# Self product as a fifth seven-block relation, first products run between the norms, projection splits on GpSimd

## What is computed

```python
def layer0(h):
    h = h @ W + b; adj = symmetric 0/1 matrix of the edges + eye, rows divided by their sums
    cur, out = h, w[0] * h
    for i in range(3):
        cur = adj @ cur
        out = out + w[i + 1] * cur
    return relu(out)

def layer1(x):
    total = sum over r of (x[src] @ W_rel[r] + b_rel[r]) * (weight where edge_type == r)
    agg = segment_sum(total, dst) / max(deg, 1)
    h = x @ W_self + b_self + agg
    x1 = layer_norm(x + h) * g1 + be1
    return layer_norm(x1 + gelu(x1 @ W1 + b1) @ W2 + b2) * g2 + be2

x = x + layer0(relu(norm(x)))
x = x + layer1(relu(norm(x)))
x = x + layer2(relu(norm(x)))     # one graph convolution
x = x + layer3(relu(norm(x)))     # two mean-aggregating convolutions
```

## Time and profile before

| | us |
|---|---|
| median of three runs | 345.9 |
| the profiled execution's own time | 345.88 |
| its span in the trace | 343.6 |
| TensorE matmul busy | 336.5 (98%) |
| VectorE busy | 243.2 (71%) |
| GpSimd busy | 153.0 (45%) |
| ScalarE busy | 87.1 (25%) |

### The profile page before, as it was taken

The page is one execution under the profiler, slowest core; times in us unless marked ns, Lnnn a source line. Parts: engine busy times, 40 slices in busy tenths (PEclk is TensorE's granted clock), DMA queues, the critical chain, the costliest instruction groups (busy, mean ns, idle before and its releaser), DMA issues.

```text
span 343.6 us, 4413 instructions
## 1 busy us (share of the span) xinstructions
PE 336.5 (98%) x1624; PEld 239.5 (70%) x1625; DVE 243.2 (71%) x428; ACT 87.1 (25%) x187; POOL 153.0 (45%) x122
## 2 busy tenths in 40 slices
PE   7999999999999999999999999999999999999996
PEld 3459887785478888888888888844774544474455
DVE  5899999988596898691484598786676555443543
ACT  3565664333410000000001062223352331112110
POOL 6000000461379999999936220491115440772020
PEclk9999999999999999999999999999999999999999
DMA  7100002728800000062300089942000000000003
GB/s 240 66 1 2 5 2 85 284 57 216 279 0 2 0 1 0 2 245 65 59 0 2 0 283 190 139 141 73 1 2 0 1 0 0 2 0 0 2 0 124
DMA packets 18630, 22.07 MB, mean 64 GB/s; under 512 B 2032, under 2 KB 10992, under 8 KB 18608
## 3 DMA queue, kind: packets, MB, share of 16 engines
q1 hardware_dynamic: 17936, 20.72, 21.6%
q0 software_dynamic: 240, 0.79, 0.8%
q10 hardware_dynamic: 432, 0.26, 0.2%
HBM read 20.72 MB, written 1.05 MB: 63 GB/s over the span
## 4 chain that ended last, share of the span: by engine, by line
PE 88%; DVE 8%; ACT 1%; DMA 1%; issue 1%; ACTq 0%; DVEq 0%
PE bank L1887 14%; PE bank L1736 14%; PE bank L1679 14%; PE bank L1616 8%; PE bank L1776 7%; PE bank L1843 6%; PE bank L1927 4%; PE bank L603 4%; PE bank L576 4%; PE bank L1875 4%; PE bank L600 3%; PE bank L1603 2%; PE bank L592 2%; DMA bias<-in_edge_type 1%; DVE stats L1209 1%; DVE h L1241 1%
## 5 line engine op out<-in xcount | busy, mean ns | idle before, releaser
L1051 ACT ACTIVATE columns<-mean_var,eps 128x1 f32<-128x1 f32 x16 | 4.7, 292 | 109.4 <-DVE mean_var L1210 109.3
L1736 PE MATMUL bank<-slots,wall 128*128 128x256 f32 x128 | 30.2, 380 | 0.0
L603 PE MATMUL bank<-slots 128*128 128x112 bf16 x256 | 27.8, 228 | 0.0
L907 POOL TENSOR_TENSOR slots<-slots 128x512 f32<-128x512 f32 x1 | 1.3, 1293 | 58.7 <-DMA slots<-in_L_gnn_W_rel 58.7
L1736 PEld LDWEIGHTS bank<-slots,wall 128*128 128x128 f32 x128 | 24.2, 190 | 3.2
L600 PE MATMUL bank<-slots 128*128 128x140 bf16 x128 | 26.2, 242 | 0.0
L386 DVE TENSOR_TENSOR slots<-slots 128x1792 bf16<-128x1792 bf16 (+1 forms) x27 | 25.0, 979 | 0.0
L1679 PE MATMUL bank<-slots,h_t 128*128 128x256 f32 x104 | 24.5, 380 | 0.0
L603 PEld LDWEIGHTS bank<-slots 128*128 128x128 bf16 x256 | 22.5, 103 | 2.7
L1887 PE MATMUL bank<-wall,h_t 128*128 128x512 f32 x48 | 22.4, 596 | 0.4 <-ACT slots L1160 0.4
L1679 PEld LDWEIGHTS bank<-slots,h_t 128*128 128x128 f32 x104 | 19.7, 190 | 3.1 <-issue 0.5
(11 more groups left out here) (293 smaller groups left out, 799.6 us busy)
## 6 DMA issues: line engine op xcount, KB each, us to landing
slots<-in_L_gnn_W_rel SPq DMA_DIRECT2D x4, 1024.0 KB, 9.6
spare<-in_L_gnn_W_ffn SPq DMA_DIRECT2D x1, 2048.0 KB, 8.0
slots<-in_L_gnn_W_ffn SPq DMA_DIRECT2D x1, 2048.0 KB, 9.1
slots<-in_L_gnn_Wr SPq DMA_DIRECT2D x8, 256.0 KB, 9.1
x<-in_x SPq DMA_DIRECT2D x4, 256.0 KB, 5.7
bias<-in_L_gnn_W SPq DMA_DIRECT2D x2, 512.0 KB, 5.0
slots<-in_L_gnn_W_self SPq DMA_DIRECT2D x1, 1024.0 KB, 5.3
bias<-in_L_gnn_b_rel SPq DMA_DIRECT2D x4, 256.0 KB, 8.4
```

The lines of the kernel that those rows point to most:

```text
L603: ins = pe.matmul(place[:, :, 0:R, 0:WIDE].rearrange("p h r d -> p r h d"), low, wgt_hot[:, s, v, a, :, :, j], start=False, stop=False, sk ...
L1736: ins = pe.matmul(into, left[:, k, tile(p)], right[:, k, :], start=(n in (0, 2, 3, 5) and r == 0 and k == 0), stop=False, skip_group_check ...
```

## The change

- The self product becomes relation 0 of five (`RELS = R + 1`), made from seven block products like the others; its result goes to a new buffer `own_out`, which shares its memory with `cnt_r`. VectorE adds it to `h` at the end of the relations (four instructions, `own_added`), and ScalarE's copies into `cnt_r` wait for that. `bself` is added as a relation's bias, so GpSimd's four additions go, and so do the four `keep_self`.
- Of the first three relations (`AHEAD = 3`) P1 and P2, which need node tiles 0 and 1 only, run on TensorE between the transposes of tiles 1, 2 and 3; `first_half(q, m)` is P1 for one output tile. Each has a bank of its own (0, 1, 2), and they share banks 3, 6 and 7 for the rest. The rest has the order P5, P6, P7, P4, P3 for relation 0 and P6, P7, P5, P4, P3 for 1 and 2. VectorE takes P1 out with `keep_right(q)`: for 0 and 1 behind tile 2's norm, for 2 behind tile 3's.
- `split_projection` of tiles 1, 2 and 3 moves from VectorE to GpSimd (`proj_split`), ahead of `combine_rel(0)`; VectorE waits for all three ahead of the inverse row sums.
- `combine_rel(0)` is now that of `wself`, whose load is the first of the three, and writes to slot 0 instead of 7. `combine_rel(1)` to `(4)` follow behind the node sums in a new order with `add_weights` and `combine_messages`.
- In the third hop `(0, 3)` is done one place earlier; `add_hop(2, 3)` stands behind tile 0's scale and shift instead of ahead of it.
- The degree product moves from the end of pass `r == 1` to the end of pass `r == 3`.
- The rows of `bself` and `brel` are loaded ahead of the five other rows.

```diff
@@ hops and projection splits @@
-                split_projection(1)
...
+            pool.wait_ge(late_kept, LATE_COUNTS)
+            for m in range(1, NT):
+                pool.wait_ge(proj_out, m + 1)
+                pool.tensor_tensor(lo[0][:, m, :], h[:, m, :], hi[0][:, m, :].bitcast(F32), ALU.subtract).then_inc(proj_split, 1)
             combine_rel(0)
             finish_build()
-            pool.wait_ge(rows_loaded, 16 * 6)
-            for t in range(NT):
-                pool.wait_ge(t_ready, use_of(H_REL, t) + 1)
-                pool.tensor_tensor(h[:, t, :], h[:, t, :], bself, ALU.add).then_inc(self_biased, 1)
             pool.wait_ge(hop_ready, HOPS * NT)
-            pool.wait_ge(node_s_ready, 3)
+            pool.wait_ge(node_s_ready, SUMS)
...
-            for t in range(2):
-                symmetric(t)
-            for t in range(2, NT):
+            for t in range(NT):
                 symmetric(t)
-                split_projection(t)
+            dve.wait_ge(proj_split, NT - 1)
             dve.wait_ge(adj_ready, NT)
...
-                    order = [(0, 0), (0, 1), (0, 2), (1, 0), (1, 1), (0, 3), (1, 2), (1, 3)]
+                    order = [(0, 0), (0, 1), (0, 2), (1, 0), (0, 3), (1, 1), (1, 2), (1, 3)]
@@ norm behind the hops, VectorE @@
+            def keep_right(q):
+
+                dve.wait_ge(rel_rows_loaded, 16 * RELS)
+                dve.wait_ge(msg_ready, rel_made(q, P1))
+                dve.tensor_tensor(quarter(rel_out[q], 0, 1), rel_parts(q)[0], rel_sides(q)[1], ALU.add).then_inc(msg_out, 1)
...
                 moments(TO_REL, m, x[:, m, :])
+                scale_and_shift(TO_REL, m)
                 if m == 0:
                     add_hop(HOPS - 1, NT - 1)
-                scale_and_shift(TO_REL, m)
+                if m == 2:
+                    keep_right(0)
+                    keep_right(1)
+            keep_right(2)
@@ relations, TensorE @@
-            pe.wait_ge(wself_loaded, 16)
-            for m in range(NT):
-                transposed(H_REL, m)
-                pairs = rows_by(wself, m)
-                product(main[m][:], pairs[:KT - 1], stop=False)
-                if m + 1 < NT:
-                    fill_h(H_REL, m + 1, h_ready[TO_REL])
-                product(main[m][:], pairs[KT - 1:], start=False).then_inc(self_ready, 1)
...
+            pe.wait_ge(acc_ready, HOPS * NT + 1)
+            for q in range(2):
+                pe.wait_ge(wrel_loaded[q], 16)
+            transposed(H_REL, 0)
+            first_half(0, 0)
+            first_half(1, 0)
+            fill_h(H_REL, 1, h_ready[TO_REL])
+            pe.wait_ge(wrel_loaded[2], 16)
+            first_half(2, 0)
+            transposed(H_REL, 1)
+            first_half(0, 1)
+            first_half(1, 1)
+            fill_h(H_REL, 2, h_ready[TO_REL])
+            first_half(2, 1)
+            second(0)
+            second(1)
+            fill_h(H_REL, 3, h_ready[TO_REL])
+            second(2)
+            for q in range(RELS):
...
+                    elif n == P4:
+                        pe.wait_ge(msg_out, rel_step(q, 3))
+                        pe.wait_ge(rel_t_ready, 4 * q + 4)
+                        block_product(p74, a22, t4, False)
@@ aggregation @@
-                if r == 1:
+                if r == R - 1:
                     pe.wait_ge(wgt_add, NT * (R - 1) + 3)
@@ GpSimd, behind the node sums @@
+            combine_rel(1)
+            combine_rel(2)
             add_weights(1)
+            combine_rel(3)
...
-            combine_rel(2)
+            add_weights(2)
+            combine_rel(4)
             combine_messages(0)
-            add_weights(2)
-            combine_rel(3)
             combine_messages(1)
             add_weights(3)
             combine_messages(2)
+            combine_messages(3)
@@ the end of the relations, VectorE @@
+            for t in range(NT):
+                dve.tensor_tensor(h[:, t, :], h[:, t, :], own_out[:, t, :], ALU.add).then_inc(own_added, 1)
```

More of the change, by code:

```diff
@@ L59 @@
 GROUPS = 4
+RELS = R + 1
+AHEAD = 3
 ADDS = 8
@@ L98, in gnn_program @@
             cnt_b = between.enter_context(nc.sbuf_tensor("cnt_b", [P, NT, N], BF16))
+        with ExitStack() as between:
+            own_out = between.enter_context(nc.sbuf_tensor("own_out", [P, NT, D], F32))
         cnt_r = sb("cnt_r", [P, NT, N], F32R)
@@ L1665, in _ @@
                         hop(m, s)
-            pe.wait_ge(wself_loaded, 16)
-            for m in range(NT):
-                transposed(H_REL, m)
-                pairs = rows_by(wself, m)
-                product(main[m][:], pairs[:KT - 1], stop=False)
-                if m + 1 < NT:
-                    fill_h(H_REL, m + 1, h_ready[TO_REL])
-                product(main[m][:], pairs[KT - 1:], start=False).then_inc(self_ready, 1)
-            def block_product(bank, left, right, fresh):
-                for m in range(2):
-                    for k in range(2):
-                        ins = pe.matmul(bank[:, m * HALF:(m + 1) * HALF], left[:, k, tile(m)], right[:, k, :],
-                                        start=fresh and m == 0 and k == 0, stop=False, skip_group_check=True)
-                ins.then_inc(msg_ready, 1)
@@ L1683, in _, with half_product @@
             a11, a12, a21, a22 = (quarter(h_t, j, i) for i in range(2) for j in range(2))
             s1, s2, s4 = node_s
-            for r in range(R):
-                b11, b12, b21, b22 = (quarter(wrel[r], i, j) for i in range(2) for j in range(2))
-                t1, t2, t4 = rel_t[r]
-                before, now = STEPS * (r - 1), STEPS * r
-                if r == 2:
+            def half_product(bank, left, right, m, fresh):
+                for k in range(2):
+                    ins = pe.matmul(bank[:, m * HALF:(m + 1) * HALF], left[:, k, tile(m)], right[:, k, :],
+                                    start=fresh and m == 0 and k == 0, stop=False, skip_group_check=True)
+                return ins
@@ new lines, in block_product, with first_half, second @@
+            def block_product(bank, left, right, fresh):
+                half_product(bank, left, right, 0, fresh)
+                half_product(bank, left, right, 1, fresh).then_inc(msg_ready, 1)
+            def first_half(q, m):
+                ins = half_product(rel_bank[q][0], a11, quarter(rel_weight[q], 0, 0), m, True)
+                if m == 1:
+                    ins.then_inc(msg_ready, 1)
+            def second(q):
+                pe.wait_ge(msg_out, rel_step(q, 1))
+                block_product(rel_bank[q][0], a12, quarter(rel_weight[q], 1, 0), False)
```

225 lines of the change are left out of this document (119 added, 106 removed).

## The result

The changed kernel takes 352.35 us (median of 4 runs, 351.40 to 354.67) against 346.02 before (4 runs), a ratio of 1.0192 with a 95% interval of 1.0141 to 1.0244. Forecast were 348.3 us and a range of 346.6 to 350.2. The kernel is slower, as forecast, but by 6.3 us instead of 2.4.

The account below looks back on a forecast made before the run. TensorE was taken as the bound (98% busy), except VectorE ahead of hop 2. From 345.9: +2.7 (steps 1, 2), -0.65, -2.0, +2.4, +0.1 give 348.4; following the clock through gave 348.3, which was taken; range 346.6 to 350.2 us.

Parts of the forecast that it names:

- Step 1: Start of the hops: three splits moved to GpSimd let VectorE start `weigh_projection` at 61.77 instead of 62.02; 0.25 us gained.
- Step 2: Ahead of hop 2: GpSimd's `combine_rel(0)` runs beside `weigh_projection` and blocks three of VectorE's four weighings; 3.0 us lost.
- no blocking: Rival ahead of hop 2: weighings go ahead of GpSimd or end before the load lands; no loss, 345.3 us; chance 12%.
- a smaller block: Rival ahead of hop 2: load lands 0.5 later, only two weighings blocked; 347.3 us; counted inside the main case's 72%.
- Step 3: Behind hop 3: earlier pair (0, 3) and later `add_hop(2, 3)` bring the first transpose at 80.02, not 80.67; 0.65 us gained.
- Step 4: TensorE's work: sixteen matmuls of 512 columns go, twenty-eight of 256 come; 2.0 us gained.
- 5a to 5f: Waits added at tile 1, the `h_t` copy, tiles 2 and 3, P7 to P4 of relation 0, degree product; 2.4 us lost.
- Step 5f: Degree product: its readers stand right behind it, so it takes 1.54 us with the wait instead of 0.92; 0.62 lost.
- Work hidden: Added work claimed to have cover, such as four `own_added` additions in idle VectorE time; GpSimd's sums close, 0.1 us charged.
- GpSimd late: Rival at the degrees: GpSimd's last weight sum comes behind `combine_messages(3)` and TensorE waits; 350 to 351 us; chance 6%.
- the clock falls: Rival in the pause ahead of hop 2: TensorE's clock drops to 1.2 GHz, up to 3.7 us more, 350 to 352; 10%.
- main case: Whole kernel: two to three weighings blocked, waits 0.6 either way; 346.9 to 349.0 us; chance 72%.

## Why the prediction was right and wrong

- **Step 1, splits on GpSimd: right.** Three in 3.77 us, 1.26 each. The weighings start at 61.84 (61.77 forecast).
- **Step 2, three blocked weighings: right**, 2.91 us instead of 2.7 at source tile 3 of hop 2. The rivals *no blocking* and *a smaller block* are wrong: 3.08 us is three blocked. The rule of the Trainium skill that stood beside it (SBUF — State Buffer, "Who interferes with whom") holds for VectorE's queued, independent instructions too, at a price of 1.04 for each. That is less than the 1.29 of a GpSimd instruction alone. So by these times the lock is not for the whole of both.
- **Step 3: right.** The first transpose is 2.28 us later (82.95 against 80.67), that is 0.63 gained, with 0.65 forecast.
- **Step 4 and 5a to 5f: nearly right.** The transposes come 3.76, 3.18 and 4.97 us apart, as the forecast clock has them (3.76, 3.16, 4.91). P4 of relation 0 starts 0.94 late (0.92 forecast), 0.78 of it listed as a wait, and the degree product takes 1.45 (1.54). But to the start of `p = 1` the loss is 3.57 where 2.3 was forecast. Of the 1.2 missing 0.2 are step 2. The relations, from the first transpose on, are 1.2 longer than forecast: 0.1 are the transposes, 0.1 the slower product behind the wait in relation 0, 0.8 the wait in relation 2, and 0.2 I can't place. The first half of the aggregation, with the degree product, is 0.2 shorter than forecast. The wait in relation 2 has no term in step 5: the step looks at TensorE's order, and finds P5 as cover between P7 and P4, but not that VectorE has `sum_weights(0, 0)`, at 1.64 beside GpSimd's new `combine_rel(3)`, ahead of both steps. The run with the sum moved shows it.
- **Step 5f and "Work hidden": the step that failed.** 5f priced the moved degree product as a wait of TensorE, 0.62 (0.50 measured). It did not follow what stands behind the degrees on VectorE: the whole of `p = 0`'s steps, norms and out-degrees. The paragraph on hidden work asked of each added instruction whether it had cover, not of the moved wait who was queued behind it. It also followed GpSimd only to its last sum of the weights (173.28, with 0.8 to spare, so that the rival *GpSimd late* is wrong), and not to its next instructions, which VectorE then meets. The runs showed 2.58 us lost there, in `p = 1`, to which the sum gave nothing: in the trace (32.83 instead of 30.25 us), and in two runs that take it away in different ways. What the paragraph did name as hidden was hidden: the four `own_added` took 6.77 us without a wait behind them. Its sum for GpSimd is slightly off: 95.8 and 47 times 1.5 and 4 are 170.3, not 169.9, and so behind the 170.05 and not ahead of it. GpSimd's time from the first to the last of these sums came out as worked out, 74.35 us.
- **The rival "the clock falls": right, in a part of the executions.** It had 10% as a case of its own, with 350 to 352. The runs show it not as a case of its own but as a chance in each run, added to the main case; the sum gave it nothing. Of the changed kernel's nine runs five are below 1.0, and the profiled one is not, so that the sum of its trace ends 0.95 short of the median. The estimate of 8 to 16 pairs at 0.92 came from no row; the one profile with a fall has seven at 0.86, which cost 2.4 us at the first transpose instead of up to 3.7. The advice of the Trainium skill against long pauses that was quoted with it (TensorE: Matmul & The Clock Gate, "Why this matters for your kernels") is borne out by the runs with the pause filled: none of 10 is below 1.0. But the pause brings the fall only in a part of the executions: 2.85 us cost nothing in one profile and a fall in another.

The sum with the measured terms starts from the 2.3 us forecast for the start of `p = 1`. To it come 0.2 in step 2, 1.2 in the relations, 0.2 less in the first half of the aggregation, and 2.6 in `p = 1`. Behind that 0.15 less are lost (6.15 us late at 208.37, 6.0 at the end of the span), and around the span 0.5 less. That makes 5.5, as between the two profiled executions (5.52). The other 0.95, up to the median, are put down to the clock, by the steps between the runs and by the runs with the pause filled; the one run of 350.43 shows that it is not the only thing that varies.

## What to carry to other kernels

When a wait is moved to a later place, list everything queued behind it on the engine that waits, to the end of the stage, and lay it beside what the other engine does at the new time. Here 7.7 us of idle time of VectorE in `p = 1` (5.48 and 2.25) were used up by two things together: a start that was 4.15 us late (7.72, less TensorE's own 3.57), and a chain that was 6.7 us longer beside GpSimd. Where VectorE has a chain on the path, keep GpSimd's instructions on SBUF out of it with a wait on that chain: one wait for each place gave 2.8 and 2.6 us here, and cost nothing, because GpSimd's results were wanted much later. And count a pause of some us that a change opens ahead of a burst of matmuls twice: once for its length and once as a chance of a fall of the clock, which a single profile may not show.

## What the runs showed of the hardware

- The same pause of TensorE, behind a hop of dense matmuls, ended with the clock at 1.0 in three profiled executions (2.82, 2.83 and 2.85 us) and at 0.50 in a fourth (2.85 us), for 14 matmuls. The runs of one kernel fall into steps of 0.005 of the mean clock. From 1.0 to 0.995 it is 1.2 us in the changed kernel, 1.4 with the additions held (the run of 346.91 left aside) and 0.9 with the degree product where it was. Dummy matmuls in the pause took the steps away in all 10 runs.
- Four of VectorE's instructions on two SBUF tensors, queued one behind the other, took 5.82 us beside GpSimd's and 2.74 alone; GpSimd's took up to 1.71 us instead of 1.29. VectorE's instructions with one of the two inputs in PSUM were not slowed: in the changed kernel two of L1288 took 1.40 us beside GpSimd's L937, from 67.59 on, and 1.41 with GpSimd idle, from 73.17 on.
- Two runs at the full clock were faster than their like: 350.43 of the changed kernel (1.0 below) and 346.91 of the one with the additions held (2.0 below). That is one and two blocked weighings' worth, and would fit a load of `wself` that lands later; neither has a profile, so it stays open.
